# Moving the record scatters and the turning of rows by a unit in a sparse graph-attention kernel

## The chip, the cores and the metric

The kernel runs on one core of a Trainium2 chip. The metric is the device time of one execution in microseconds. The engines are TensorE (PE; its weight loads are PEld), VectorE (DVE), ScalarE (ACT), GpSimd (POOL) and SyncE (SP), which here issues transfers alone.

## The reference

A transformer convolution over a graph of 8192 nodes with a dense 0/1 adjacency matrix, and a layer norm over the sum with its input:

```python
q = (x @ Wq + bq).reshape(n, H, C)        # n = 8192, H = 4, C = 32
k, v = ...                                 # the same with Wk, bk and Wv, bv
attn = einsum('nhc,mhc->hnm', q, k) / sqrt(C)
alpha = softmax of attn over the m with adj[n, m] != 0
out = einsum('hnm,mhc->hnc', alpha, v), transposed to (n, C * H)
x_r = x @ Ws + bs
beta = sigmoid(concat([out, x_r, out - x_r]) @ Wb)
y = layernorm(x + beta * x_r + (1 - beta) * out)
```

The first rows of the matrix are full of edges, the later ones nearly empty, so the number of neighbours falls with the node number.

## The kernel before

Nodes are in 64 tiles of 128. Tile 0 is worked densely, in 40 small "pieces" strewn over the run. All others go by lists: the key and value rows of all nodes are computed first and stored in memory (`kv_rows`, 1 KB a row), and for each node only the rows of its neighbours are gathered.

**Units.** A tile's list of slots is cut into chunks of at most 24 slots; a chunk is a unit. There are 76: tile 1 has units 0 to 3 (19, 19, 18, 18 slots), tile 2 units 4 to 6, tile 3 units 7 and 8, tile 4 units 9 to 11, tile 5 units 12 and 13, tile 6 units 14 and 15 (14 and 13 slots), tile 7 unit 16 (23), tile 8 units 17 and 18, tile 9 units 19 and 20, and from there on tiles have one unit, but for tile 16. All engines run through the same list of units, each in an order written out in its own block, and meet by semaphores.

**In a unit.** POOL issues one indirect gather for each slot (L743) into a ring of 60 slots of `kv`; it waits on `summed` where a slot is still in use. DVE multiplies by the query and reduces (L1134, L1136), takes words, and after ACT's exponential (L978) weighs the values (L1156). PE sums them (L923). DVE finishes a tile in the next tile's first unit.

**Scan.** The lists come from the adjacency matrix. Along with the units, one later tile a unit is scanned: SP loads its four parts of 1 MB into a ring of five (L571, `load_adj`; each waits until ACT has masked the part five before), ACT turns them to masks (L945), PE packs them into words (L773), DVE takes the largest words out (L1167 to L1174). Unit k scans tile k + 4 on DVE, and k + 5 on ACT and PE.

**Records.** Within a window of tiles nodes are ranked by degree and change places. Windows are tiles 2 and 3 (window 0), 4 to 7 (window 1), 8 to 15 (window 2), then eight tiles each. A record holds a node's row of `x`, its list and its number. When the spots are known (`find_spots`, L1276, in unit 5 for window 1, in unit 13 for window 2), POOL scatters a window's records to memory, one indirect transfer a tile (L715), and SP loads them back by tile (L577, `load_record`) in a unit given by `load_plan`: never ahead of the scatter's unit, and not over four tiles ahead of use. A record load also waits until the store of the tile ten before has landed. POOL stores a finished tile six tiles behind (L723).

**Turning.** For the query of tile p + 1, PE transposes its rows (`turn_rows`, L795), ACT copies them (`copy_xs`, L969), PE multiplies them by the weights (`project_qr`, L800, L801), ACT copies a part (`copy_r`, L973). DVE waits for that in the first unit of tile p + 1.

**Dense pieces.** SP loads 0.5 MB of `x` columns (L581) two units ahead of a group of pieces, and one unit after its begin the values (L585) and a stretch of the adjacency matrix, `d_in` (L588), for which DVE waits in `mark_piece` (L1343). All SP loads are in one queue, in this order in a unit: `place_x` (L565, the `x` part of records, two windows ahead), records, dense loads, adjacency parts of the scan.

Of the kernel before, what the change touches and what calls it, by code (L numbers as in the profile page):

```python
# [16 lines left out]
T = N // P  # L17
# [20 lines left out]
WINDOWS = [[2, 3], [4, 5, 6, 7]] + [list(range(t, t + 8)) for t in range(8, T, 8)]  # L38
# [48 lines left out]
def chunks(p):  # L87
    n = -(-SLOTS[p] // MAX_S)
    return [SLOTS[p] // n + (c < SLOTS[p] % n) for c in range(n)]


def n_chunks(p):
    return len(chunks(p))
# [3 lines left out]
UNIT_OF = {pc: k for k, pc in enumerate(UNITS)}  # L97
# [4 lines left out]
def half(k):  # L102
    return (SIZES[k] + 1) // 2
# [68 lines left out]


def scatter_plan():
    at = {2: 0}
    for k, w in KEYS_AT.items():
        last = UNIT_OF[WINDOWS[w][0] - 1, 0] - (w > 1)
        if w + 2 < len(WINDOWS):
            last = min(last, LISTED_AT[WINDOWS[w + 2][0]] - 1)
        at[min(k + 6, last)] = w  # L180
    return at


SCATTER_AT = scatter_plan()


# [48 lines left out]
def heads_begun(k):  # L235
    return sum(h is not None for u, (c, h) in PIECE_AT.items() if u < k)
# [60 lines left out]
def sparse_tiles(nc, x, adj, Wq, bq, Wk, bk, Wv, bv, Ws, bs, Wb, kv_dram, x_cols, rec_dram, late_dram, ident, gate_w, eps_col, tile_list,  # L297
                 n_dense, n_late, w_all, b_row, bk_col, bq_col, ones, out):
    ctx = ExitStack()
    with ctx:  # L300
# [232 lines left out]
        def need(eng, sem, value):  # L533
            if value > 0:
                eng.wait_ge(sem, value)
# [217 lines left out]
        def _(pe):  # L753
# [11 lines left out]
            def pack_part(t, h):  # L765
                w, k = ps_w[t % 2], part_no(t, h)
                if h == 0:
                    need(pe, words_checked, t - 2)
                    nc.tensor.matmul(w[:], place_w[:], place[:], start=True, stop=False)
                pe.wait_ge(masked, k + 1)  # L770
                for s in range(SLABS_A_PART):
                    slab = h * SLABS_A_PART + s
                    last = nc.tensor.matmul(w[:], bit_w[:, slab], mask[:, k % 2, s * WORD:(s + 1) * WORD],  # L773
                                            start=False, stop=(slab == SLABS - 1))
                last.then_inc(part_packed, 1)
# [5 lines left out]
            def spread_keys(w):  # L781
                n = len(WINDOWS[w])
                pe.wait_ge(diag_ready, w + 1)
                pe.wait_ge(d_q_ready, 1)
                need(pe, ranked, w)
                for b in range(0, n, 4):
                    m = min(n - b, 4)
                    last = nc.tensor.matmul(ps_key[:, b * P:(b + m) * P], ones_sq[:],  # L788
                                            diag[:, b:b + m].rearrange("p a c -> p (a c)"), start=True, stop=True)
                last.then_inc(keys_spread, 1)  # L790

            def turn_rows(p):
                pe.wait_ge(rec_loaded[p % RECS], rec_loads(p))
                need(pe, xs_ready, p - 1)
                nc.tensor.transpose(ps_x[:, 0:P], rec_in[:, p % RECS, 0:D], ident[:]).then_inc(rows_turned, 1)  # L795

            def project_qr(p):
                pe.wait_ge(xs_ready, p)
                need(pe, q_used, p - 2)
                nc.tensor.matmul(ps_q[p % 2][:, 0:2 * D], ones[:], b_row[0:1, 2 * D:4 * D], start=True, stop=False)  # L800
                nc.tensor.matmul(ps_q[p % 2][:, 0:2 * D], xs[:, p % 2], w_all[:, 2 * D:4 * D], start=False,  # L801
                                 stop=True).then_inc(q_ready, 1)
# [21 lines left out]
            def turn_piece(k):  # L824
                c, h = PIECE_AT[k]
                pe.wait_ge(d_expd, head_no(c, h) + 1)
                for b in range(DKEYS // P):
                    last = nc.tensor.transpose(ps_key[:, b * P:(b + 1) * P], d_e[:, b * P:(b + 1) * P], ident[:])  # L828
                last.then_inc(d_turned, 1)

            def sum_piece(k):
                c, h = PIECE_AT[k]
                pe.wait_ge(d_wT_ready, head_no(c, h) + 1)
                pe.wait_ge(d_v_loaded, 16 * (c + 1))
                for b in range(DKEYS // P):
                    last = nc.tensor.matmul(ps_key[:, 0:C], d_wT[:, b * P:(b + 1) * P], d_v[:, b, h * C:(h + 1) * C],
                                            start=(b == 0), stop=(b == DKEYS // P - 1))
                last.then_inc(d_summed, 1)
# [60 lines left out]
            spread_keys(0)  # L899
            pack_words(4)  # L900
            for k, (p, c) in enumerate(UNITS):
                if c == 0 and p + 1 < T:
                    turn_rows(p + 1)
                scan = k in SCAN_AT and SCAN_AT[k] + 1 < T
                if scan:
                    pack_part(SCAN_AT[k] + 1, 0)
                    pack_part(SCAN_AT[k] + 1, 1)
                if c == 0 and p + 1 < T:
                    project_qr(p + 1)
                if k in RANK_AT:  # L910
                    need(pe, d_copied, heads_begun(k))
                    spread_keys(RANK_AT[k])
                if k in PIECE_AT:
                    begin_piece(k)
                if scan:
                    pack_part(SCAN_AT[k] + 1, 2)
                    pack_part(SCAN_AT[k] + 1, 3)
                piece = k in PIECE_AT and PIECE_AT[k][1] is not None
                if piece:
                    turn_piece(k)  # L920
                pe.wait_ge(weighted, k + 1)
                for s in range(SIZES[k]):
                    last = nc.tensor.matmul(acc[:, c * D:(c + 1) * D], ident[:], kv[:, START[k] + s, D:2 * D],  # L923
                                            start=(s == 0), stop=(s == SIZES[k] - 1))
                    if s in (half(k) - 1, SIZES[k] - 1):
                        last.then_inc(summed, 1)
                if piece:
                    sum_piece(k)
                if k == OVER_AT:
                    pe.wait_ge(over_ready, 1)  # L930
                    pe.wait_ge(ranked, len(WINDOWS))
                    pe.wait_ge(d_copied, H * DCHUNKS)
                    nc.tensor.matmul(ps_key[0:1, 0:T], one_col[:], over[:], start=True, stop=True).then_inc(over_summed, 1)
                if k == LOOP_AT:
                    fallback()

        @block.scalar
        def _(act):
# [117 lines left out]
            for s in range(SLABS):  # L1056
                last = nc.scalar.mul(bit_w[:, s], ident[:], float(CODE << s))
# [16 lines left out]
            for k, (p, c) in enumerate(UNITS):  # L1074
                t = SCAN_AT.get(k, T)
                scan = t + 1 < T
                if scan:
                    mask_part(t + 1, 0)
                    mask_part(t + 1, 1)
                if c == 0 and p + 1 < T:  # L1080
                    copy_xs(p + 1)
                begun, ended = PIECE_AT.get(k), PIECE_AT.get(k - 1)
                if ended and ended[1] is not None:
                    copy_sums(k - 1)
                exp_chunk(k)
                if k and UNITS[k - 1][1] == 0 and UNITS[k - 1][0] > 1:
                    normalize(UNITS[k - 1][0] - 1)
                if scan:
                    mask_part(t + 1, 2)
                    mask_part(t + 1, 3)  # L1090
                if begun and begun[1] is None:
                    copy_keys(k)
                if c == 0 and p > 1:
                    gate_exp(p - 1)
                if c == 0 and p + 1 < T:
                    copy_r(p + 1)
                if begun and begun[1] is not None:
                    exp_piece(k)
                if t < T:
                    check_words(t)  # L1100
                if begun and begun[1] is not None:
                    copy_turned(k)
                n = n_chunks(p)
                if n > 1 and c == n - 1:
                    r = p % 2
                    act.wait_ge(below_ready, multi_upto(p))
                    nc.scalar.activation(share[:, r, 0:n], below[:, r, 0:n], ACT.Exp, scale=SCALE).then_inc(share_ready, 1)
                if k in RANK_AT:
                    rank_window(RANK_AT[k])
                if k == JOIN_AT:  # L1110
                    act.wait_ge(d_low_ready, 1)
                    nc.scalar.activation(d_share[:], d_share[:], ACT.Exp).then_inc(d_share_ready, 1)
                if k == JOIN_AT + 1:
                    finish_first()
                if k == LOOP_AT:
                    fallback()
# [475 lines left out]
```

## Time and profile before

| | us |
|---|---|
| median of 3 timed runs | 1698.73 (1697.92 to 1701.44) |
| the profiled execution, own time | 1692.9 |
| its span, first to last instruction | 1691.1 |
| mean granted TensorE clock in it | 0.747 |

Rows of the timeline give start, duration, engine, line, operation, tile written and tile read, and in brackets the idle time of the engine just before and what ended it. "issue" is time in which the engine waited for nothing that the profile shows. The busy time of SP rows spans all transfers merged in a row.

### The profile page before, as it was taken

The page shows a single profiled execution, that of the slowest core. Times are in us where ns is not written, and L with a number is a line of the kernel's source. Part 1 is how long each engine was busy: PE and PEld are TensorE (multiplying, and loading weights), DVE is VectorE, ACT ScalarE, POOL GpSimd, SP SyncE. Part 2 cuts the span into 40 slices and gives each one's busy share as a digit, 9 for nine tenths or more (in the row PEclk, how much of TensorE's full clock was granted, in tenths as well). Part 3 has the DMA queues.
Part 4 walks back from the last instruction along what each step waited for, and adds up shares of the span by engine and source line. Part 5 has one row for each costly group of instructions (what it writes and reads, how often), then busy time and mean ns, then how long its engine had stood idle before and what let it go on. Part 6 is the DMA issues. An engine that isn't in the chain of part 4 may idle for free.

```text
span 1691.1 us, 19935 instructions
## 1 busy us (share of the span) xinstructions
PE 1037.8 (61%) x4648; PEld 641.3 (38%) x4708; DVE 1317.6 (78%) x3330; ACT 834.6 (49%) x1581; POOL 1203.5 (71%) x1745
## 2 busy tenths in 40 slices
PE   7405555577564365676767766776777784454564
PEld 5202323354342233343434443443454342243353
DVE  4887888889876388877867777886886888887585
ACT  2305434346645145654565657674866685331222
POOL 5265774777667776677777777777777777777774
PEclk9656767778786678777877787777787787766575
DMA  9758976769786477787699878988799798333431
GB/s 357 288 213 319 278 264 225 261 223 331 261 316 236 172 249 281 275 322 254 246 334 326 299 266 317 350 301 324 296 352 331 284 340 302 107 95 111 108 101 53
DMA packets 129220, 438.45 MB, mean 259 GB/s; under 512 B 25319, under 2 KB 60606, under 8 KB 96334
## 3 DMA queue, kind: packets, MB, share of 16 engines
q1 hardware_dynamic: 74718, 297.15, 47.4%
q0 software_dynamic: 53808, 135.83, 25.3%
q10 hardware_dynamic: 576, 4.19, 0.6%
q8 instruction: 38, 0.62, 0.1%
q14 instruction: 80, 0.66, 0.1%
HBM read 417.69 MB, written 19.44 MB: 258 GB/s over the span
## 4 chain that ended last, share of the span: by engine, by line
DVE 29%; POOL 28%; issue 16%; DVEq 9%; PE 7%; DMA 6%; ACT 3%; SPq 0%; ACTq 0%; POOLq 0%
POOL s_kv L743 24%; DVE s_raw L1136 4%; DVE s_kv L1134 4%; DVE s_wtop L1174 3%; DMA s_d_in<-in_adj 3%; DVEq L1173 3%; DVE s_kv L1156 2%; POOL node_records L715 2%; DVE s_top L1218 2%; DVEq L1323 2%; PE s_acc L923 2%; POOL out_rows L723 2%; PE s_ps_w L773 1%; DVEq L1225 1%; DVE s_d_max L1334 1%
## 5 line engine op out<-in xcount | busy, mean ns | idle before, releaser
L743 POOL DMA_INDIRECT s_kv<-kv_rows,s_rec_in x1057 | 1053.9, 997 | 396.4 <-issue 319.3
L773 PE MATMUL s_ps_w<-s_mask,s_bit_w 128*128 128x512 bf16 x1001 | 330.6, 474 | 276.6 <-ACT s_mask L945 273.7
L945 ACT ACTIVATE s_mask<-s_adj_in 128x2048 bf16<-128x2048 f32 x252 | 477.9, 1898 | 30.4 <-PE s_ps_w L773 15.8
L923 PE MATMUL s_acc<-s_kv,ident 128*128 128x128 f32 x2114 | 326.8, 326 | 122.8 <-DVE s_kv L1156 122.6
L923 PEld LDWEIGHTS s_acc<-s_kv,ident 128*128 128x128 f32 x2114 | 318.0, 241 | 147.4 <-DVE s_kv L1156 145.1
L773 PEld LDWEIGHTS s_ps_w<-s_mask,s_bit_w 128*128 128x128 bf16 x1008 | 102.6, 112 | 470.4 <-ACT s_mask L945 349.8
L1134 DVE TENSOR_TENSOR s_kv<-s_kv,s_ps_q 128x1792 f32<-128x1792 f32 (+17 forms) x76 | 152.7, 2009 | 74.9 <-DMA s_kv<-kv_rows,s_rec_in 73.1
L978 ACT ACTIVATE s_ps_q<-s_sc 128x56 f32<-128x56 f32 (+17 forms) x76 | 16.9, 222 | 347.9 <-DVE s_sc L1147 347.9
L1136 DVE TENSOR_REDUCE s_raw<-s_kv 128x56 f32<-128x1792 f32 (+17 forms) x76 | 152.6, 2007 | 5.6
L1156 DVE TENSOR_TENSOR s_kv<-s_kv,s_ps_q 128x1792 f32<-128x1792 f32 (+17 forms) x76 | 152.2, 2003 | 5.7 <-ACT s_ps_q L978 3.7
L1174 DVE MAX8 s_wtop<-s_words 128x8 f32<-128x512 f32 x171 | 118.8, 695 | 14.8 <-issue 1.3
L818 PE MATMUL s_ps_key<-s_d_kT,s_d_qT 32*128 32x512 f32 x128 | 83.6, 736 | 67.4 <-DVE s_d_pen L1343 67.4
L715 POOL DMA_INDIRECT node_records<-s_rec,s_spot x62 | 61.6, 993 | 53.0 <-DVE s_spot L1276 35.0
L969 ACT COPY s_xs<-s_ps_x 128x128 f32<-128x128 f32 x63 | 16.3, 259 | 151.4 <-PE s_ps_x L795 151.2
L723 POOL DMA_INDIRECT out_rows<-s_yout,s_rec_in x63 | 64.6, 1026 | 26.8 <-issue 17.7
L962 ACT ACTIVATE s_diag<-s_ps_key,s_neg_key 128x1024 bf16<-128x1024 f32 (+2 forms) x62 | 66.1, 1066 | 28.1 <-PE s_ps_key L788 23.8
L828 PE MATMUL s_ps_key<-ident,s_d_e 128*128 128x128 f32 x256 | 49.0, 354 | 46.8 <-ACT s_d_e L1009 46.8
L1218 DVE MAX8 s_top<-s_cand 128x8 f32<-128x72 f32 (+6 forms) x234 | 62.4, 267 | 17.5 <-issue 1.5
L1170 DVE MATCH_REPLACE8 s_words<-s_wtop,s_words 128x512 f32<-128x512 f32 x108 | 73.0, 676 | 0.0
L1009 ACT ACTIVATE s_d_e<-s_ps_key,s_d_shift 128x1024 f32<-128x1024 f32 x32 | 35.6, 1114 | 74.1 <-DVE s_d_shift L1336 74.1
L828 PEld LDWEIGHTS s_ps_key<-ident,s_d_e 128*128 128x128 f32 x256 | 39.1, 183 | 69.0 <-ACT s_d_e L1009 68.9
L800 PE MATMUL s_ps_q<-b_row,ones 1*128 1x256 f32 x126 | 49.3, 473 | 18.1 <-ACT s_xs L969 18.1
(258 smaller groups left out, 1469.1 us busy)
## 6 DMA issues: line engine op xcount, KB each, us to landing
s_adj_in<-in_adj SPq DMA_DIRECT2D x248, 1024.0 KB, 8.1
s_kv<-kv_rows,s_rec_in POOLq DMA_INDIRECT x1057, 5.6
kv_rows<-s_kv SPq DMA_DIRECT2D x16, 512.0 KB, 7.6
s_rec_in<-node_records SPq DMA_DIRECT2D x62, 106.0 KB, 6.7
s_kv<-in_x_cols SPq DMA_DIRECT2D x4, 1024.0 KB, 8.5
s_adj_in<-in_adj ACTq DMA_DIRECT2D x4, 1024.0 KB, 15.8
s_d_in<-in_x_cols SPq DMA_DIRECT2D x8, 512.0 KB, 8.9
s_d_v<-kv_rows SPq DMA_DIRECT2D x8, 512.0 KB, 10.2
```

Source lines behind the costliest of these rows:

```text
L715: nc.gpsimd.indirect_dma_start(out=rec_dram[:, :], out_offset=bass.IndirectOffsetOnAxis(ap=spot[:, t:t + 1], axis=0), in_=rec[:, w % 2, j] ...
L723: nc.gpsimd.indirect_dma_start(out=out[:, :], out_offset=bass.IndirectOffsetOnAxis(ap=rec_in_u[:, r, NODE_AT:NODE_AT + 1], axis=0), in_=y_ ...
L743: nc.gpsimd.indirect_dma_start(out=kv[0:n, START[k] + s], out_offset=None, in_=kv_dram[:, :], in_offset=bass.IndirectOffsetOnAxis(ap=rec_i ...
L773: last = nc.tensor.matmul(w[:], bit_w[:, slab], mask[:, k % 2, s * WORD:(s + 1) * WORD], start=False, stop=(slab == SLABS - 1))
L828: last = nc.tensor.transpose(ps_key[:, b * P:(b + 1) * P], d_e[:, b * P:(b + 1) * P], ident[:])
L923: last = nc.tensor.matmul(acc[:, c * D:(c + 1) * D], ident[:], kv[:, START[k] + s, D:2 * D], start=(s == 0), stop=(s == SIZES[k] - 1))
L945: nc.scalar.activation(mask[:, q % 2], adj_in[:, q % ADJ_RING], ACT.Sign, accum_out=edges[:, t, h:h + 1]).then_inc(masked, 1)
L1134: nc.vector.tensor_tensor(part, part, ps_q[r][:, 0:D].unsqueeze(1).to_broadcast([P, s, D]), ALU.mult)
L1136: nc.vector.tensor_reduce(raw[:, 0:s * H].rearrange("p (s h) -> p s h", h=H), part.rearrange("p s (h c) -> p s h c", h=H), AX, ALU.add)
L1156: nc.vector.tensor_tensor(v, v, e_sh.unsqueeze(3).to_broadcast([P, s, H, C]), ALU.mult).then_inc(weighted, 1)
L1174: nc.vector.max(got[:, 8 * k:8 * k + 8], words[:])
L1218: nc.vector.max(got[:, 8 * k:8 * k + 8], all_cand)
```

## The change

Three windows are scattered one unit later, in the unit just ahead of the window's own first unit: window 0 in unit 3 (was 2), window 1 in unit 8 (was 7), window 2 in unit 16 (was 15). The record loads of `load_plan` follow: tiles 4 to 7 in SP's unit 8 (was 7), tiles 8 to 10 in unit 16 (was 15). The places of all later windows stay. The turning of the next tile's rows with its copies goes from a tile's first unit to its last; where a tile has one unit nothing moves.

```diff
 def scatter_plan():
-    at = {2: 0}
+    at = {UNIT_OF[2, 0] - 1: 0}
     for k, w in KEYS_AT.items():
-        last = UNIT_OF[WINDOWS[w][0] - 1, 0] - (w > 1)
+        last = UNIT_OF[WINDOWS[w][0], 0] - 1
         if w + 2 < len(WINDOWS):
             last = min(last, LISTED_AT[WINDOWS[w + 2][0]] - 1)
         at[min(k + 6, last)] = w
...
             for k, (p, c) in enumerate(UNITS):
-                if c == 0 and p + 1 < T:
+                ends = c == n_chunks(p) - 1 and p + 1 < T
+                if ends:
                     turn_rows(p + 1)
...
-                if c == 0 and p + 1 < T:
+                if ends:
                     project_qr(p + 1)
...
-                if c == 0 and p + 1 < T:
+                ends = c == n_chunks(p) - 1 and p + 1 < T
+                if ends:
                     copy_xs(p + 1)
...
-                if c == 0 and p + 1 < T:
+                if ends:
                     copy_r(p + 1)
```

## Rows read from the trace of the kernel before

**Rows 1.** The page, part 1: busy time, share and instructions of each engine.

```profile
PE 1037.8 (61%) x4648; PEld 641.3 (38%) x4708; DVE 1317.6 (78%) x3330; ACT 834.6 (49%) x1581; POOL 1203.5 (71%) x1745
```

**Rows 2.** The page, part 5: groups; busy, mean ns, idle before and releaser.

```profile
L743 POOL DMA_INDIRECT s_kv<-kv_rows,s_rec_in x1057 | 1053.9, 997 | 396.4 <-issue 319.3
...
L800 PE MATMUL s_ps_q<-b_row,ones 1*128 1x256 f32 x126 | 49.3, 473 | 18.1 <-ACT s_xs L969 18.1
```

**Rows 3.** Timeline of POOL, 60 to 600 us.

```profile
131.40 1.02 POOL L715 DMA_INDIRECT node_records<-s_rec,s_spot  x1 [10.71 <-DVE s_spot L1276]
...
163.12 0.99 POOL L743 DMA_INDIRECT s_kv<-kv_rows,s_rec_in  x1 [5.88 <-PE s_acc L923]
...
269.22 0.88 POOL L743 DMA_INDIRECT s_kv<-kv_rows,s_rec_in  x1 [7.50 <-PE s_acc L923]
...
283.42 1.04 POOL L715 DMA_INDIRECT node_records<-s_rec,s_spot  x1 [12.12 <-DVE s_spot L1276]
...
338.93 1.03 POOL L743 DMA_INDIRECT s_kv<-kv_rows,s_rec_in  x1 [0.30 <-issue]
...
472.11 1.03 POOL L715 DMA_INDIRECT node_records<-s_rec,s_spot  x1 [12.15 <-DVE s_spot L1276]
...
575.22 1.03 POOL L723 DMA_INDIRECT out_rows<-s_yout,s_rec_in  x1 [0.30 <-issue]
```

**Rows 4.** Waits of POOL, whole run: total us, times, longest.

```profile
POOL s_kv L743 <- PE s_acc L923: 31.8, 9, 9.2
```

**Rows 5.** Timeline of POOL, 680 to 700 us.

```profile
692.30 1.00 POOL L743 DMA_INDIRECT s_kv<-kv_rows,s_rec_in  x1 [9.23 <-PE s_acc L923]
```

**Rows 6.** Timeline of DVE, 60 to 600 us.

```profile
151.65 2.69 DVE L1156 TENSOR_TENSOR s_kv<-s_kv,s_ps_q 128x2432 f32<-128x2432 f32 x1 [2.16 <-ACT s_ps_q L978]
...
221.15 0.75 DVE L1343 TENSOR_SCALAR s_d_pen<-s_d_in 128x1024 bf16<-128x1024 f32 x1 [0.19 <-DMA s_d_in<-in_adj]
...
375.00 2.42 DVE L1134 TENSOR_TENSOR s_kv<-s_kv,s_ps_q 128x2176 f32<-128x2176 f32 x1
...
420.53 1.23 DVE L1334 TENSOR_REDUCE s_d_max<-s_ps_key 128x1 f32<-128x1024 f32 x1 [0.34 <-PE s_ps_key L820]
...
503.86 1.89 DVE L1134 TENSOR_TENSOR s_kv<-s_kv,s_ps_q 128x1664 f32<-128x1664 f32 x1 [4.08 <-DMA s_kv<-kv_rows,s_rec_in]
...
584.19 0.69 DVE L1343 TENSOR_SCALAR s_d_pen<-s_d_in 128x1024 bf16<-128x1024 f32 x1 [22.56 <-DMA s_d_in<-in_adj]
```

**Rows 7.** Timeline of SP, 60 to 600 us.

```profile
138.46 0.97 SPq L577 DMA_DIRECT2D s_rec_in<-node_records  x2
...
195.84 5.05 SPq L588 DMA_DIRECT2D s_d_in<-in_adj  x1
...
305.90 5.18 SPq L577 DMA_DIRECT2D s_rec_in<-node_records  x4
...
577.59 0.33 SPq L577 DMA_DIRECT2D s_rec_in<-node_records  x1
```

**Rows 8.** Timeline of PE, 140 to 160 us.

```profile
150.70 0.47 PE L795 MATMUL s_ps_x<-ident,s_rec_in 128*128 128x128 f32 x1 [11.54 <-DMA s_rec_in<-node_records]
```

**Rows 9.** Windows: length, busy by engine (instructions), PEclk, DMA share, GB/s.

```profile
120.00:132.00 12.00, 1.62 (x3) 0.66 (x3) 8.00 (x33) 2.89 (x6) 1.29 (x2) 0.50 0.07 22
...
138.00:144.00 6.00, 0.98 (x3) 0.31 (x4) 4.36 (x9) 3.85 (x5) 4.77 (x5) 0.86 1.00 365
```

**Rows 10.** The page, part 6: issues, KB each, us to landing.

```profile
s_adj_in<-in_adj SPq DMA_DIRECT2D x248, 1024.0 KB, 8.1
```

**Rows 11.** The page, part 3: packets, MB, share of 16 engines' span.

```profile
q0 software_dynamic: 53808, 135.83, 25.3%
```

**Rows 12.** Timeline of SP, 312 to 340 us.

```profile
322.83 9.30 SPq L571 DMA_DIRECT2D s_adj_in<-in_adj  x4
```

**Rows 13.** All record loads of L577, whole run.

```profile
DMA to landing us min/median/max: 2.1/6.7/17.7
```

**Rows 14.** Timeline of SP, 500 to 532 us.

```profile
512.28 2.22 SPq L571 DMA_DIRECT2D s_adj_in<-in_adj  x2
```

## The prediction

> **What bounds the kernel now.** I read the page first. Its busy shares [rows 1] name DVE (1317.6 us) ahead of POOL (1203.5 us), so they would send the reader to DVE. The timeline of POOL corrects this. POOL works off one list: 1057 gathers, 62 scatters, 63 stores, each about 1.0 us busy with 0.3 us of issue behind it [rows 2]; that is 1182 x 1.3 = 1537 us, and the list starts at 71 us. So POOL is occupied almost without a hole, and its holes are worth listing. Three of them stand before the first scatter of a window, which waits for the spots that DVE computes: 10.71, 12.12 and 12.15 us [rows 3]. The waits for buffers (PE's sums) make 31.8 us in nine pieces [rows 4]; the last is the one of 9.23 us that ends at 692.30 [rows 5], and from there the list runs to the end. What moves that gather moves the end, one for one.
>
> Next I asked what sets 692.30. From 131 us on DVE waits for no gather until unit 15, where it waits 4.08 us (503.86) [rows 6], so from 472.11 on POOL sets the pace. At 575.22 POOL issues the store of tile 2 [rows 3]; SP stands before the record load of tile 12 until that store has landed (577.59) [rows 7], behind it is the adjacency piece `d_in`, and DVE waits 22.56 us for it, to 584.19 [rows 6]. From there DVE is busy up to the wait at 692.30. So the chain is: POOL's list at 472.11, store, SP, `d_in`, DVE, POOL again. Between 131 and 472 us the reverse holds: DVE is nearly without a hole, and POOL is the one that waits.
>
> **The change, part by part: the scatters.** Nothing is removed; the places are, by unit: window 0 from 2 to 3, window 1 from 7 to 8, window 2 from 15 to 16. Later windows keep theirs (k + 6 is the smaller number there).
>
> *Window 2.* POOL now issues the 13 gathers of unit 15 where it waited 12.15 us. They take 13 x 1.3 = 16.9 us and their buffers have been free since unit 11. The wait goes whole: -12.15 us, and unit 16 starts that much sooner. For every us by which POOL reaches unit 15 later than now, one us of it is lost.
>
> *Window 1.* The 12.12 us go too (19 of unit 7's 20 gathers need only unit 4). From the last wait of unit 6 (269.22) it would work through units 6 to 8 and reach unit 9, tile 4, at about 327 instead of 338.93 [rows 3]. This gains nothing by itself: unit 15 is after the records of tile 4, and they are what is late next, below.
>
> *Window 0.* POOL gathers unit 2 at 121 to 144.4 (18 x 1.3), and scatters at 144.4 instead of 131.4. Unit 3 then needs the first sums of unit 0.
>
> **The turning of rows.** `turn_rows(2)` stands today ahead of all of unit 0 on PE, and waits 11.5 us for records to 150.70 [rows 8]; ACT's `copy_xs(2)` and its exponential stand behind it, and DVE waits 2.16 us for that [rows 6]. With the turning in unit 3 DVE is 2.15 us earlier. Nine turnings move (tiles 2 to 7, 9, 10 and 17, each behind a tile of several units). Each is a transpose, two products (the first takes 49.3 us for 63 tiles, so 0.8 us each [rows 2]) and two ACT copies: under 2 us of PE, covered by DVE's long units. The one place without cover is unit 11, where DVE already waits 0.34 us for PE's scores [rows 6]: +1.7 us there, on DVE only.
>
> **What SP does meanwhile.** Behind the record loads of tiles 2 and 3 SP has `place_x(2)`, the dense columns, and all adjacency loads from number 21 on. They get through at 138.46 now, 5.7 us after the second scatter starts at 132.7 [rows 7]; they will at 145.8 + 5.7 = 151.5, 13 us later. ACT and PE have loaded parts for that time, but the DMA engines don't: their share is 1.00 at 138 to 144 [rows 9], and the half megabyte issued at 195.84 is still 25.3 us on its way [rows 6, 7]. The last loads issued before SP stops should be in by about 148 (one takes 8.1 us [rows 10], and they queue); the next bytes come at about 153. About 5 us of DMA time are lost. Given back are the gathers of unit 2, of which 10 now run at 121 to 132, where the engines are 0.07 busy [rows 9]; less what POOL gains later about 5 gathers fewer lie before the critical load, at 0.253 x 1691 / 1182 = 0.36 us each [rows 11] that is 1.9 us. The critical load is the first `d_in` of adjacency: issued 195.84, used 221.15, with 0.19 us to spare [rows 6, 7]. I put its landing 5.0 - 1.9 = 3.1 us later, and DVE's and SP's clock from there on at +3.1 us instead of -2.15. Bounds: -2.15 (the load is in time) and +8 (no relief, the 5 us lost, and 3 us more because what moves behind gathers then moves slowly, as that load's 25.3 us show).
>
> **Records of tile 4.** Their loads move from SP's place for unit 7 to that for unit 8, that is past four adjacency loads that wait for ACT. Today they are issued at 305.90 [rows 7]; the four loads they move behind are at 322.83 to 332.1 [rows 12], so with `place_x(3)` they start at 332.6. The line's landing times are 2.1, 6.7 and 17.7 us (least, median, most) [rows 13]; with two whole adjacency parts just ahead I take 9.0. That is 341.6, against 338.93 for POOL's unit 9 today: POOL is 2.7 us late there, plus the 3.1. The bounds: +0.4 at the median, +11.4 at the most. POOL's gain of 12 us from window 1 is spent entirely in this wait. DVE is not touched by this: it comes to unit 9 at 375.00 [rows 6], when its 17 gathers (22 us) are long in.
>
> [...]
>
> **Records of tile 8.** They too move past four adjacency loads, whose last goes out at 514.2 [rows 14]. It waits for ACT, ACT for DVE's unit 15, and that loses its wait of 4.1 us for gathers: the record load goes at 514.2 + 0.4 - 4.1 + 3.1 + 1.7 = 515.3 and lands at 524.3. POOL comes to unit 17 today at 472.11 + 45 x 1.3 = 530.6 (8 scatters, 36 gathers, a store), so at 530.6 - 12.15 + 5.8 = 524.2. 0.1 us.
>
> **Sum.** -12.15 + 3.1 + 2.7 + 0.1 = -6.2 us, at unit 17. After this the order of work is that of today, the store of tile 2 and all behind it come 6.2 us earlier, and so does the end. The profiled execution took 1692.9 us with a span of 1691.1; it would take 1686.7. The runs timed have a median of 1698.73, 5.8 us above it; the same step from there gives 1692.5 us.
>
> **Rivals.** (a) The dense load is in time after all, and the records land at the median: -12.15 - 2.15 + 0.4 + 0.3 = -13.6 us, 1685.1. For it: the engines idle before 132, and the transfer has slack that the trace can't show. Against: 0.19 us of slack on DVE. (b) The move is a wash: SP's 13 us of silence cost 8 us at the dense load, and tile 4's records take 11 us: -12.15 + 8 + 4.7 = +0.5, 1699.3. The busy shares speak for such a result too, read simply: DVE is the fullest engine, so waits of POOL cost nothing. The Trainium skill (Perfetto Trace Analysis, Identifying Performance Opportunities) says to take the engine of highest occupancy first; by that rule the change leaves the time at 1698.7. The issue gaps, which busy time leaves out, speak against it. (c) Slower: SP's ring is so full at unit 9 that the records take the 17.7 us that this line has shown once, on top of the late dense load: -12.15 + 8 + 11.4 + 0.4 = +7.7 us, 1706.4. It decides from the point where the two delays exceed 12.15 us together. Against it: at 305 to 340 the adjacency loads are paced by ACT, not by the ring.
>
> **How the numbers follow.** Forecast 0.42, (a) 0.22, (b) 0.20, (c) 0.16. The measurement tells 0.2%, 3.4 us, from nothing. Faster by more: all of (a), nine tenths of the forecast, a little of (b): 0.61. Slower by more: (c) and a little of (b): 0.18. Within: 0.21. The range runs from (a) with its record loads a little quicker, 1684, over the forecast's 1692.5, to the upper side of (b), 1701; what is left out is (c) and the edges. The forecast's own range is 1688 to 1697.
>
> **What the changed profile would show.** No wait of POOL on `s_spot` above 1 us; a wait of some 14 us of POOL at unit 9 for tile 4's records, its first gather at 342 to 347; SP's record loads at about 151, 335 and 513; the first `s_d_pen` after a wait of 3 to 6 us, instead of 0.19; scatter of window 2 starting at 480 to 484; unit 16 done 5 to 9 us earlier, and so the gather now at 692.30; POOL without a hole from there. I am wrong if `s_d_pen` shows no wait (then (a)), if POOL waits more than 20 us at unit 9, if PE's `turn_rows` blocks unit 16, or if DVE's long stretch before 692 doesn't move with the store of tile 2.

## The result, and the profile after

The changed kernel takes 1692.94 us (median of 12 runs, 1692.02 to 1695.27) against 1699.74 us for the kernel before (12 runs, 1695.23 to 1703.59) on the same chip: a ratio of 0.9957, 95% interval 0.9947 to 0.9968, or 7.3 us less (5.4 to 9.0). A second measurement of both kernels gave 0.995 (0.9937 to 0.9963). The forecast was 1692.5 us. Ratios and spreads leave out runs over 1.5% above a kernel's fastest (one of 1770.21 us in experiment 2, two of the kernel before in experiment 7).

The profiled execution of the changed kernel took 1695.27 us with a span of 1693.4, so beside the profile of before (1692.9, span 1691.1) it looks 2.3 us slower. That contradiction is the first thing to clear up, and a second profile of the unchanged kernel does it (first experiment). Here are the rows that answer to those of before (the edit makes the file longer, so L924, L1136, L1278, L1336 and L1345 are L923, L1134, L1276, L1334 and L1343 of the kernel before). First the timeline of GpSimd (POOL) in the changed kernel:

```profile
144.55 1.02 POOL L715 DMA_INDIRECT node_records<-s_rec,s_spot  x1 [0.30 <-issue]
...
156.61 1.04 POOL L743 DMA_INDIRECT s_kv<-kv_rows,s_rec_in  x1 [9.72 <-PE s_acc L924]
...
304.66 1.02 POOL L715 DMA_INDIRECT node_records<-s_rec,s_spot  x1 [0.31 <-issue]
...
347.31 1.03 POOL L743 DMA_INDIRECT s_kv<-kv_rows,s_rec_in  x1 [13.54 <-DMA s_rec_in<-node_records]
...
485.54 1.02 POOL L715 DMA_INDIRECT node_records<-s_rec,s_spot  x1 [0.30 <-issue]
...
530.73 1.03 POOL L743 DMA_INDIRECT s_kv<-kv_rows,s_rec_in  x1 [4.04 <-DMA s_rec_in<-node_records]
...
575.65 1.04 POOL L723 DMA_INDIRECT out_rows<-s_yout,s_rec_in  x1 [0.30 <-issue]
...
693.65 1.00 POOL L743 DMA_INDIRECT s_kv<-kv_rows,s_rec_in  x1 [9.60 <-PE s_acc L924]
```

The three waits for spots ahead of the scatters (10.71, 12.12 and 12.15 us in [rows 3]) are gone. Three longer waits stand in their place: GpSimd waits for TensorE's sums at 156.61 (9.72 us, where window 0's wait was), for the records of tile 4 at 347.31 (13.54 us, where window 1's was) and for those of tile 8 at 530.73 (4.04 us). For window 2's 12.15 us only this last one stands, and it is smaller. All waits for sums together grow from 31.8 us [rows 4] to 52.0.

The timeline of VectorE (DVE), the same run, at the rows of [rows 6]. The `s_d_pen` rows are `mark_piece`, which waits for the dense adjacency load `d_in`:

```profile
228.15 0.74 DVE L1345 TENSOR_SCALAR s_d_pen<-s_d_in 128x1024 bf16<-128x1024 f32 x1 [9.27 <-DMA s_d_in<-in_adj]
...
429.54 1.22 DVE L1336 TENSOR_REDUCE s_d_max<-s_ps_key 128x1 f32<-128x1024 f32 x1 [2.94 <-PE s_ps_key L820]
...
585.00 0.69 DVE L1345 TENSOR_SCALAR s_d_pen<-s_d_in 128x1024 bf16<-128x1024 f32 x1 [22.93 <-DMA s_d_in<-in_adj]
```

And that of SyncE (SP), at the rows of [rows 7]:

```profile
153.27 1.04 SPq L577 DMA_DIRECT2D s_rec_in<-node_records  x2
...
204.77 1.60 SPq L588 DMA_DIRECT2D s_d_in<-in_adj  x1
...
339.51 2.89 SPq L577 DMA_DIRECT2D s_rec_in<-node_records  x4
...
520.19 11.52 SPq L577 DMA_DIRECT2D s_rec_in<-node_records  x4
```

The record loads sit where the forecast put them (about 151, 335 and 513 us), 2 to 7 us later. The first `s_d_pen` now has 9.27 us of wait where [rows 6] show 0.19, and starts 7.0 us later. Read against that one profile this says that the late dense load cost 7 us. A second profile of the kernel before puts the same row at 226.94 us, later than in one of the two profiles of the changed kernel, so that reading doesn't stand; what the load's place did cost is taken up in experiment 2.

### The profile page after: what moved, and what is told of

The parts are those of the page before. It is cut to its first block, busy times and chain, and to the rows that moved or that the text cites. A ratio compares the mean times of both kernels' runs of the same rounds, so it can differ in the third digit from the quotient of the medians.

```text
span 1693.4 us, 19995 instructions
## 1 busy us (share of the span) xinstructions
PE 1065.1 (63%) x4708; PEld 646.7 (38%) x4708; DVE 1315.9 (78%) x3330; ACT 834.4 (49%) x1581; POOL 1205.2 (71%) x1745
## 4 chain that ended last, share of the span: by engine, by line
POOL 34%; DVE 24%; issue 17%; DVEq 8%; DMA 7%; PE 7%; ACT 3%; SPq 0%; POOLq 0%; ACTq 0%
POOL s_kv L743 29%; DVE s_raw L1138 3%; DVE s_kv L1136 3%; DVE s_wtop L1176 3%; DVEq L1175 3%; DMA s_d_in<-in_adj 3%; POOL node_records L715 2%; DMA s_adj_in<-in_adj 2%; POOL out_rows L723 2%; DVE s_kv L1158 2%; PE s_acc L924 2%; DVE s_top L1220 1%; PE s_ps_w L773 1%; DVEq L1325 1%; DVE s_d_max L1336 1%
## 5 line engine op out<-in xcount | busy, mean ns | idle before, releaser
L773 PE MATMUL s_ps_w<-s_mask,s_bit_w 128*128 128x512 bf16 x1008 | 341.5, 484 | 271.7 <-ACT s_mask L946 271.4
L946 ACT ACTIVATE s_mask<-s_adj_in 128x2048 bf16<-128x2048 f32 x252 | 478.0, 1899 | 62.2 <-DMA s_adj_in<-in_adj 48.2
L924 PE MATMUL s_acc<-s_kv,ident 128*128 128x128 f32 x2114 | 327.1, 326 | 112.5 <-DVE s_kv L1158 112.2
L924 PEld LDWEIGHTS s_acc<-s_kv,ident 128*128 128x128 f32 x2114 | 318.2, 241 | 138.9 <-DVE s_kv L1158 136.5
L773 PEld LDWEIGHTS s_ps_w<-s_mask,s_bit_w 128*128 128x128 bf16 x1008 | 102.8, 113 | 479.3 <-ACT s_mask L946 358.9
L1136 DVE TENSOR_TENSOR s_kv<-s_kv,s_ps_q 128x1792 f32<-128x1792 f32 (+17 forms) x76 | 152.7, 2009 | 73.2 <-DMA s_kv<-kv_rows,s_rec_in 71.2
L1220 DVE MAX8 s_top<-s_cand 128x8 f32<-128x72 f32 (+6 forms) x234 | 62.3, 266 | 17.5 <-issue 1.5
```

The costliest lines, as they stand in the source:

```text
L946: nc.scalar.activation(mask[:, q % 2], adj_in[:, q % ADJ_RING], ACT.Sign, accum_out=edges[:, t, h:h + 1]).then_inc(masked, 1)
L1136: nc.vector.tensor_tensor(part, part, ps_q[r][:, 0:D].unsqueeze(1).to_broadcast([P, s, D]), ALU.mult)
```

## The experiments

All ratios are to the kernel before, run in turn with it on the same chip. Where times of the changed kernel's trace are compared, they are those of its second profile (experiment 1), unless said otherwise. The changed kernel was not timed beside experiments 3 to 6, which ran on another chip than 1 and 2, so a difference of theirs to the changed kernel is one of two ratios, each with its own interval.

**1. Both kernels once more.** No edit; the control.

> The kernel before, unchanged, for a second profiled execution. Theory A (the first profiled execution, 1692.9 us, was a quick one by chance, and its chain is otherwise typical): timed ratio 1.000, profiled execution at 1697 to 1701; the 5 to 8 us are then found at one or two transfers. Rival B (the profiler shortens this kernel): profiled execution again near 1693, and the chain the same to a microsecond.

> The changed kernel, unchanged, for a second profiled execution. In the first one POOL's unit 17 began at 530.73, against 530.37 in the kernel before, though the timed runs are 7 us quicker. Theory A: timed ratio 0.996, the wait of DVE for the first adjacency piece (9.27 us) and the waits for records (13.54 and 4.04 us) come back within 3 us each. Rival B: these waits differ widely from execution to execution (by more than 5 us), and the timed gain is where they are short.

Measured: the kernel before against itself 1.0007 (0.9991 to 1.0024); the changed kernel 0.995 (0.9937 to 0.9963), 1690.45 us to 1697.48. The two new profiles have spans of 1701.1 and 1689.2 us. This is the pair to compare; the timelines of the kernel before, second profile, VectorE and then SyncE:

```profile
226.94 0.69 DVE L1343 TENSOR_SCALAR s_d_pen<-s_d_in 128x1024 bf16<-128x1024 f32 x1 [5.87 <-DMA s_d_in<-in_adj]
...
509.66 1.89 DVE L1134 TENSOR_TENSOR s_kv<-s_kv,s_ps_q 128x1664 f32<-128x1664 f32 x1 [4.06 <-DMA s_kv<-kv_rows,s_rec_in]
```

```profile
201.76 0.79 SPq L588 DMA_DIRECT2D s_d_in<-in_adj  x1
```

The same program, unchanged, has 5.87 us of wait at the first `s_d_pen` in one execution and 0.19 in the other. Why, its ScalarE (ACT) timeline shows, here the second profile of the kernel before:

```profile
178.99 1.91 ACT L945 ACTIVATE s_mask<-s_adj_in 128x2048 bf16<-128x2048 f32 x1 [2.64 <-DMA s_adj_in<-in_adj]
...
185.67 1.91 ACT L945 ACTIVATE s_mask<-s_adj_in 128x2048 bf16<-128x2048 f32 x1 [4.68 <-DMA s_adj_in<-in_adj]
...
192.69 1.91 ACT L945 ACTIVATE s_mask<-s_adj_in 128x2048 bf16<-128x2048 f32 x1 [3.03 <-DMA s_adj_in<-in_adj]
...
198.82 1.91 ACT L945 ACTIVATE s_mask<-s_adj_in 128x2048 bf16<-128x2048 f32 x1 [4.12 <-DMA s_adj_in<-in_adj]
```

Between 150 and 205 us the adjacency parts arrive later than ScalarE wants them (six waits, 18.0 us in sum; the first profile has one, of 3.60 us, at 201.32). SyncE gets to the dense load at 201.76 instead of 195.84 [rows 7], and the 6 us stay: tile 4's first gather starts at 344.7 (338.93 in [rows 3]) and the last wait for sums ends at 700.97 (692.30 in [rows 5]). The profile on which the forecast was built was of an execution in which that stream of loads ran ahead. Neither profile of the kernel before is a typical one: its timed runs have medians of 1695.91 to 1699.74, the first profiled execution (1692.9) is quicker than every timed run of the result above, and the second (1702.89) is the slowest of its ten.

The rows of the changed kernel's second profile, GpSimd, at tile 8's first gather and at the last wait for sums:

```profile
527.19 1.03 POOL L743 DMA_INDIRECT s_kv<-kv_rows,s_rec_in  x1 [1.90 <-DMA s_rec_in<-node_records]
...
690.38 1.00 POOL L743 DMA_INDIRECT s_kv<-kv_rows,s_rec_in  x1 [9.79 <-PE s_acc L924]
```

With the second pair, milestone by milestone (us, from the timelines; the last row is the execution's span):

| | before | changed | difference |
|---|---|---|---|
| first `s_d_pen` | 226.94 | 226.13 | -0.8 |
| spots of window 1 | 288.20 | 287.29 | -0.9 |
| first gather of unit 9 (tile 4) | 344.7 | 345.66 | +1.0 |
| spots of window 2 | 476.94 | 476.90 | 0.0 |
| first gather of unit 17 (tile 8) | 536.2 | 527.19 | -9.0 |
| store of tile 2 | 581.04 | 572.02 | -9.0 |
| third dense chunk, `s_d_pen` | 590.79 | 581.20 | -9.6 |
| last wait for sums ends | 700.97 | 690.38 | -10.6 |
| span | 1701.1 | 1689.2 | -11.9 |

In this pair nothing is gained or lost up to 477 us, 9.0 us are gained between 477 and 527, and they are carried to the end through the chain that the forecast named. The pair overstates the gain, since its execution of the kernel before took longer than the median one: the spans differ by 11.9 us, against the first profile of the kernel before by only 1.9 (1691.1 to 1689.2), and the timed runs (7.3 and 8.5 us) lie between. So the pair shows where the gain is made, and the timed runs how large it is.

**2. The windows apart.** Windows 1 and 2 later, window 0 back in unit 2:

```
-    at = {UNIT_OF[2, 0] - 1: 0}
+    at = {2: 0}
```

> The changed kernel with window 0 scattered in unit 2 as before. Theory A (SP's silence of 13 us costs DVE 9.27 us at the first adjacency piece, and all of it reaches the end by way of tile 4's records): that wait falls below 2 us, unit 9 starts at about 339 instead of 347, and the time is 10 us below the kernel before, ratio 0.994. Rival B (the delay is made good before unit 15): as the changed kernel, 0.996.

Window 0 alone later, windows 1 and 2 back:

```
-        last = UNIT_OF[WINDOWS[w][0], 0] - 1
+        last = UNIT_OF[WINDOWS[w][0], 0] - 1 - (w in (1, 2))
```

> Windows 1 and 2 scattered as before, window 0 in unit 3, the turnings moved. Theory A: DVE waits about 9 us at the first adjacency piece and is 7 us late from there, so the spots of window 2 come at 478 instead of 471, and the time is 7 us above the kernel before, ratio 1.004. Rival B (POOL is 8 us ahead after unit 2, and DVE makes the wait good): ratio 0.998 to 1.000.

Measured: 0.9962 (0.9947 to 0.9977) and 1.0016 (1.0003 to 1.0029). Without window 0's move the gain is the same as with it, within the intervals. Window 0 and the turning alone make the kernel slower, by 2.6 us (1700.04 to 1697.48), between the two numbers expected and just clear of noise. The first `s_d_pen`, on the timelines of VectorE of the one and of the other:

```profile
227.20 0.88 DVE L1345 TENSOR_SCALAR s_d_pen<-s_d_in 128x1024 bf16<-128x1024 f32 x1 [8.49 <-DMA s_d_in<-in_adj]
```

```profile
226.72 0.74 DVE L1345 TENSOR_SCALAR s_d_pen<-s_d_in 128x1024 bf16<-128x1024 f32 x1 [7.86 <-DMA s_d_in<-in_adj]
```

SyncE issues the first record loads at 138.74 us in the first and at 153.64 in the second; the dense load lands at the same time, to 0.5 us. So in these executions SyncE's silence of 15 us costs the dense load nothing. VectorE waits 2 to 2.6 us longer there than in the kernel before (5.87 us), about the 2.15 us that the moved turning gives it.

Where the 2.6 us of the second kernel come from its profile doesn't show: the last wait for sums ends at 699.40, against 700.97 and 692.30 in the two profiles of the kernel before. The spread of the timed runs gives a hint. With window 0 in unit 2 they lie 7.0 to 10.3 us apart (the kernel before, the first kernel here, the one of experiment 3; 9 to 31 runs each). With window 0 in unit 3 they lie 3.3 to 4.9 us apart (the changed kernel twice, the second kernel here, experiments 5 and 6; 6 to 12 runs each), and 7.7 us in experiment 4, where the load itself is moved. That would fit a dense load that is in time in some executions of the kernel before, as in its first profile, and always late in the other; window 0's move would then take the quick executions away. It is not shown, and it is not all, for beside the moves of windows 1 and 2 window 0's costs nothing (1690.45 to 1691.33 us).

**3. Window 2 alone later**, windows 0 and 1 back, the turning as changed.

```
-    at = {UNIT_OF[2, 0] - 1: 0}
+    at = {2: 0}
-        last = UNIT_OF[WINDOWS[w][0], 0] - 1
+        last = UNIT_OF[WINDOWS[w][0], 0] - 1 - (w == 1)
```

> The changed kernel with windows 0 and 1 scattered where the kernel before has them (units 2 and 7); window 2 in unit 16 and the turning of rows stay changed. Theory (the whole gain is the 12 us wait of GpSimd at window 2, now filled with unit 15's gathers): GpSimd still waits 10.7 and 12.2 us at windows 0 and 1, not at window 2; the records of tile 4 are loaded by 312 us, and the time is 0.9950 to 0.9960 of the kernel before, as for the whole change, or about 1 us less than that. Rival (windows 0 and 1, or the turning of rows, carry part of the gain): 0.998 or more.

Measured: 1691.53 us to 1695.91, ratio 0.9971 (0.9958 to 0.9984). The waits of GpSimd (reason, total us, times, longest):

```profile
POOL s_kv L743 <- PE s_acc L924: 39.8, 17, 10.7
POOL node_records L715 <- DVE s_spot L1278: 22.6, 2, 11.9
```

Two waits for spots are left, the window 2 one is gone, and about two thirds of the gain are there (-4.9 us, interval -2.7 to -7.1, against -7.3). It is less than the 0.9950 to 0.9960 expected, and the intervals overlap, so whether the moves of windows 0 and 1 add 1 or 2 us to it, or nothing, is not settled by this run.

**4. The disputed term alone: the first dense load earlier.** The changed kernel, with SyncE's order in unit 2 changed:

```
-                if k - 1 in PIECE_AT and PIECE_AT[k - 1][1] is None:
+                if k - 1 in PIECE_AT and PIECE_AT[k - 1][1] is None and k - 1 > FIRST_PIECE:
                     load_dense_rows(PIECE_AT[k - 1][0])
+                if k == FIRST_PIECE:
+                    load_dense_rows(0)
```

> The changed kernel with the first dense adjacency load (L588, tile s_d_in) issued by SyncE before unit 2's adjacency loads, not behind them. This is the disputed term of the prediction (+3.1 us for a late first dense load) measured by itself. Theory A (a late load there moves all that follows on VectorE, as the 6 us between two executions of the kernel before seemed to do): VectorE's wait of 7.6 to 9.3 us at the first s_d_pen falls below 3 us, window 2's spots come 5 to 8 us earlier, and the time falls by 4 to 7 us against the changed kernel, a ratio of 0.991 to 0.993 to the kernel before. Theory B (what VectorE gains there it loses at the 22.9 us wait for the third dense load, which hangs on tile 2's store and so on GpSimd): the wait goes, and the ratio stays at 0.995 to 0.996. Rival C (the adjacency loads of unit 2 come late instead): no gain in the wait's end, 0.996 to 0.999.

Measured: 1684.26 us, ratio 0.9919 (0.9897 to 0.9941). On VectorE's timeline:

```profile
218.71 0.69 DVE L1347 TENSOR_SCALAR s_d_pen<-s_d_in 128x1024 bf16<-128x1024 f32 x1
```

The wait is gone, the row starts 7.4 us earlier than in the changed kernel's second profile (226.13), and theory A holds: the store of tile 2 comes 5.3 us earlier (566.74 to 572.02), the last wait for sums 5.0 us (685.38 to 690.38), and the time falls by about 5 us (0.995 to 0.9919 of 1696; the two intervals overlap slightly, 0.9937 and 0.9941). The way goes by VectorE's spots of window 2 (470.78 to 476.90) and by tile 4's first gather (337.50 to 345.66), and not by the third dense chunk, whose wait stays at 22.89 us and comes earlier with the store. So the forecast was right that this load sets VectorE's clock; that window 0's move delays it shows only against the quick first profile, and the timed runs of experiment 2 leave it open.

**5. The records one unit earlier in SyncE's order**, where the kernel before has them:

```
-        k = max(scattered[WINDOW_OF[p]], UNIT_OF[max(p - LEAD, 1), 0])
+        k = max(scattered[WINDOW_OF[p]] - (WINDOW_OF[p] in (1, 2)), UNIT_OF[max(p - LEAD, 1), 0])
```

> The changed kernel with SyncE's first record loads of windows 1 and 2 taken one unit earlier in its own order (units 7 and 15, where the kernel before has them), still behind the scatters' landing by their semaphore; this undoes only the term that the prediction put at +2.7 us. Theory: the records of tile 4 are loaded by 320 us, not 338; GpSimd's wait of 13.8 us at unit 9 falls to 1 to 8 us and that of 1.9 us at unit 17 goes. What is then late next is window 2's spots on VectorE at 477 us, so of the 13.8 us some 6 to 8 are kept: the time falls by 3 to 8 us against the changed kernel, a ratio of 0.991 to 0.993. Rival (the adjacency loads that now stand behind the record loads feed the marking late, and VectorE loses what GpSimd gains): 0.995 or more.

Measured: 1684.07 us, ratio 0.9922 (0.99 to 0.9944). SyncE's loads go out at 310.29 (337.60 in the changed kernel's second profile), and of GpSimd's waits for records none is left (one of 8.18 us for TensorE's sums at 401.73 is new); what is left at window 2 is, on GpSimd's timeline:

```profile
479.05 1.02 POOL L715 DMA_INDIRECT node_records<-s_rec,s_spot  x1 [1.79 <-DVE s_spot L1278]
...
681.86 1.00 POOL L743 DMA_INDIRECT s_kv<-kv_rows,s_rec_in  x1 [9.22 <-PE s_acc L924]
```

The scatter of window 2 starts 5.0 us earlier (484.02 to 479.05) and is again bound by the spots; the last wait for sums ends 8.5 us earlier (690.38 to 681.86). This is the price of the late records: about 5 us of time (0.995 to 0.9922 of 1696, with intervals that overlap slightly), of the 12 that window 1's move had won.

**6. The dense loads ahead of the record loads of the same unit.** In unit 17 this takes the third dense adjacency out from behind tile 12's record load, which waits for the store of tile 2:

```
-                for p in LOAD_AT.get(k, []):
-                    load_record(p)
                 if k + 2 in PIECE_AT and PIECE_AT[k + 2][1] is None:
                     load_dense_x(PIECE_AT[k + 2][0])
                 if k - 1 in PIECE_AT and PIECE_AT[k - 1][1] is None:
                     load_dense_rows(PIECE_AT[k - 1][0])
+                for p in LOAD_AT.get(k, []):
+                    load_record(p)
```

> The changed kernel with SyncE's dense loads (L581, L585, L588) issued ahead of the record loads of the same unit, so that in unit 17 the third dense adjacency does not stand behind tile 12's record load, which waits for the store of tile 2. Theory: VectorE's wait of 22.9 us at the second s_d_pen behind that store (584 us) falls below 10 us, and with it GpSimd's waits of 7.9 and 9.8 us for TensorE near 650 and 690 us; the time falls by 5 to 15 us against the changed kernel, a ratio of 0.986 to 0.993. Rival (VectorE is only as far as GpSimd's gathers let it be; its waits for the gathers' landing, 71.8 us in total, grow by what the wait gave back): the wait goes and the ratio stays at 0.995 to 0.996.

Measured: 1673.89 us, ratio 0.9867 (0.9845 to 0.9889), the fastest kernel of the study: 22 us below the kernel before and about 14 below the changed one. The timelines of SyncE and of VectorE:

```profile
542.10 0.62 SPq L588 DMA_DIRECT2D s_d_in<-in_adj  x1
```

```profile
561.09 0.69 DVE L1345 TENSOR_SCALAR s_d_pen<-s_d_in 128x1024 bf16<-128x1024 f32 x1
```

The load goes out at 542.10 instead of 575.25, and the wait of 22.86 us is gone. GpSimd's waits near 644, 664 and 690 us (5.6, 3.3 and 9.8 us in the changed kernel's second profile) are gone too (none above 0.4 us there), and VectorE's for gathers grow by only 3 us (71.8 to 74.9 in sum). The gather that started at 690.38 starts at 674.31, so nearly all of the 17.5 us between the two spans is made here, though the edit reorders later units as well. The largest wait on the chain was one that the change did not touch.

**7. Four kernels on a slower chip.** The edits of 4, 5 and 6 together; the kernel before with those of 4 and 6; the turning of rows moved alone (`at = {2: 0}` and `- (w in (1, 2))` in the changed kernel); window 1 alone later (`at = {2: 0}` and `- (w == 2)`).

> The changed kernel with the three edits of SyncE's order together: the first dense adjacency ahead of unit 2's adjacency loads, the record loads of windows 1 and 2 one unit earlier, and the dense loads ahead of the record loads of their unit. Alone they gave ratios of 0.9919, 0.9922 and 0.9867 where the change itself gives 0.995 to 0.9957. Theory (three separate waits of three stretches, so the gains add: 0.0034 + 0.0031 + 0.0086 beside the change's own 0.9953): 0.979 to 0.982. Rival (the dense load of unit 17 and the records of window 2 release the same stretch, and one gain swallows the other): 0.983 to 0.987. In the trace VectorE has no wait above 3 us at the first and at the third s_d_pen and GpSimd none above 3 us for records.

> The kernel before with the same two edits of SyncE's order of dense loads (its record loads of windows 1 and 2 stand in units 7 and 15 already); beside the run above this gives what the change is worth once the other waits are out of its way. Theory (the change is worth the whole of window 2's 12 us and of window 1's, where GpSimd sets the pace): 0.986 to 0.989, so that the change is worth 0.006 to 0.009 on top, more than the 0.0045 that it is worth in the kernel as it stands. Rival (what the change gives was hidden in VectorE's waits that the edits take away): within 0.003 of the run above.

> Only the second part of the change: the next tile's rows turned in a tile's last unit; all windows scattered as in the kernel before. Theory (a step of TensorE and ScalarE that GpSimd and VectorE don't wait for in either place, but for some 2 us before the keys' maximum in unit 11): 0.999 to 1.001, with that wait of 1.8 to 3 us there. Rival (the part carries some of the gain): 0.998 or less. Second rival (the 2 us in unit 11 reach the end): 1.0012 to 1.002.

> Window 1 alone scattered later (unit 8), windows 0 and 2 as in the kernel before, turning changed. This is the term of +2.7 us by itself (records of tile 4 wanted after a wait of 14 us where there were 12 at the scatter). Theory: GpSimd's wait of 12 us at window 1 goes, one of 13 to 14.5 us for the records of tile 4 stands in its place, tile 4's first gather starts 0.5 to 3 us later than in the kernel before, and the ratio is 1.000 to 1.002. Rival (the gathers brought ahead free VectorE earlier and win back what the records lose): below 0.999.

These four ran on another chip than the rest, and there the kernel before itself took 2154.27 us, 27% more than on the others. The ratios are 0.996 (0.9932 to 0.9988), 0.9983 (0.995 to 1.0017), 1.004 (1.0012 to 1.0068) and 1.0093 (1.0062 to 1.0124). None of the four is in the range that its theory gave. The expected numbers were worked out from the faster chips' profiles, so the misses say little about those chips. Why, the waits of VectorE in the kernel with the turning alone show (reason, total us, times, longest):

```profile
DVE s_divisor L1307 <- remote: 145.2, 12, 31.8
DVE s_d_max L1336 <- remote: 106.8, 9, 32.4
DVE s_top L1220 <- issue: 68.7, 47, 3.2
```

None of these is there on the other chips (1.5 us at L1220; no "remote" at all). The single instructions of GpSimd and VectorE take what they took: 997 ns for a gather, 2009 for the product at L1136; TensorE's at L773 take 500 ns, where the changed kernel's second profile has 489. Between them GpSimd, VectorE, ScalarE and TensorE stand idle with "issue" or "remote" as the reason, for which the profile names no instruction or transfer of this core, and GpSimd is no longer full: it waits 160.2 us in sum for TensorE's sums, where the changed kernel's second profile has 50.3. With the bound elsewhere, a wait removed from GpSimd should be worth less, and the kernel with all edits gains 0.4% where the change with one of them gained 1.3%; that the one is the cause of the other is not shown. What holds the instructions the profile doesn't name; it stays open. So does whether the gains of experiments 4 to 6 add up on a chip like the others, what the change is worth beside them, and what the turning of rows costs by itself there: the runs that were to tell did not. On this chip the turning alone costs 0.4%, clear of noise. On the others no run separates it from window 0's move, and the two together cost 0.16% (experiment 2), so a cost of the turning is not ruled out.

One reading can be made within this chip. Window 1 alone later is 0.7% slower than the turning alone by the medians (2177.86 to 2163.61 us), 0.5% by the ratios, whose intervals just overlap. The timelines of GpSimd at tile 4's first gather, first with window 1 later, then with the turning alone:

```profile
390.25 1.03 POOL L743 DMA_INDIRECT s_kv<-kv_rows,s_rec_in  x1 [26.25 <-DMA s_rec_in<-node_records]
```

```profile
383.90 1.02 POOL L743 DMA_INDIRECT s_kv<-kv_rows,s_rec_in  x1 [11.54 <-PE s_acc L924]
```

Two waits, of 12.91 us for spots (at 317.16) and of 11.54 for sums, are exchanged for one of 26.25 for records, and the gather starts 6.4 us later. Here the exchange loses; on the faster chips it was nearly even (12.23 for 13.79).

## Why the prediction was right, point by point

**The gain is window 2's wait: right.** Experiment 3 keeps two thirds of the gain with that window alone (with the turning moved); the milestones of experiment 1 show it between the spots of window 2 and unit 17. GpSimd did follow its list from there without a hole until the wait for sums.

**The chain to the end: right.** The 9.0 us at unit 17 are 9.0 at the store of tile 2, 9.6 at the dense chunk that waits for it, 10.6 at the last wait for sums. Experiment 6 cuts this chain at the load and wins 14 us more, which shows it the other way round. VectorE was the fullest engine by busy time, the change took waits from GpSimd, and the time fell by 0.4%. The Trainium skill (Perfetto Trace Analysis, Identifying Performance Opportunities) says to optimize the engine of highest occupancy first, which is VectorE here, with 78% to GpSimd's 71%. The measured gain of 7.3 us from GpSimd's waits doesn't agree with a plain reading of it, though experiment 6 won more at a wait of VectorE.

**+3.1 us for window 0's silence on SyncE: the term whose size the runs don't bear out.** In the second pair it measured 0 within 1 us: the first `s_d_pen` is at 226.94 in the kernel before and at 226.13, 226.72 and 227.20 in three kernels with window 0 in unit 3, in unit 3 and in unit 2. Against the first profile of the kernel before it would be 5.0 to 7.0 us (221.15 to 226.13 and 228.15). By timed runs it is nothing beside the other two moves, and with the turning alone beside it the kernel is 2.6 us slower (experiment 2). So the size is not settled. The step behind it was "with 0.19 us to spare": the load was taken as just in time, from a profile in which it was. In three of the four profiles on these chips with window 0 in unit 2 it is 6 us late (226.94, 227.20, 227.24), behind adjacency loads that are short of supply themselves, and against these the lost DMA time changes nothing. The lower bound of this term, -2.15 us, shows in none of them: VectorE's 2 us from the moved turning end up in the wait. The wait itself was 7.64 and 9.27 us, where the forecast had 3 to 6.

**+2.7 us for tile 4's records: mechanism right, size near.** The wait came (13.54 and 13.79 us; forecast some 14) and swallowed window 1's 12 us. Net, unit 9 starts 1.0 us later, not 2.7. The whole cost of their late place is larger than the term, since without it part of window 1's gain is kept: 5 us, by experiment 5. The landing time that was taken, 9.0 us, was about right: 345.66 less 337.60 is 8.1 us for the first of the four.

**+0.1 us for tile 8's records: 1.9 us** (4.04 in the first profile), because the loads went out at 516.60 and not at 515.3 and the first landed 10.6 us after that, not 9.0. GpSimd came to them at 525.3, 1.1 us later than reckoned.

**+1.7 us at unit 11: right in place and about right in size** (waits of 1.85 and 2.94 us for a forecast of some 2), and without effect on window 2's spots in the second pair (476.90 to 476.94). It isn't there in every kernel with the turning moved: the first kernel of experiment 2 and those of experiments 3 and 6 wait 0.36 to 0.45 us at that place, as the kernel before does.

**The sum** was -12.15 + 3.1 + 2.7 + 0.1 = -6.2; the second pair gives -12.0 + 0 + 1.0 + 1.9 = -9.1 at unit 17, and the timed runs -7.3 and -8.5. Window 2's scatter started at 485.54 and 484.02, where the forecast had 480 to 484. The forecast time, 1692.5, was nearer than its terms were, and in that there is luck: a base of 1698.73 that was 1 us low made up for a gain that was about 1 us small. By size the case lies between the forecast and rival (a), but none of (a)'s three parts (dense load in time, -2.15 from the turning, records at the median) came out as written: the load was waited for 7.64 us, the 2.15 us ended in that wait, and the records took 8.1 us.

## What to carry to other kernels

Before a term is built on a slack of tenths of a microsecond, look whether what feeds it has slack, and take a second profile: here a load that was just in time behind a stream of loads was 6 us late in the next execution of the same kernel, and against that execution a delay put on it cost nothing. When a wait is filled with other work, look in the same place for the next thing that the engine needs, and move its load too; here the records' loads, moved back one unit, gave about 5 us beside the change's 7. And the largest wait on the chain (22.9 us at a load queued behind another load's wait) was a matter of the order of a few lines on SyncE's queue, worth 14 us; follow the chain for such a place first.

## What the runs showed of the hardware

The same program, with the same instructions, differs by 6 us at 227 us into the run from how fast 1 MB loads arrive (ScalarE waited 3.6 us for them in one profile and 18.0 in the other between 150 and 205 us). The difference doesn't go away: it is 8.7 us at the last wait for sums, and the two profiled executions took 1692.9 and 1702.89 us. A single pair of profiles showed the sign of this change wrong (+2.3 us), while 12 timed runs of each told it within 0.1%.

On one chip all of the kernels took some 27% longer, with unchanged durations of the single instructions of GpSimd, VectorE and ScalarE (997 ns a gather, 2009 the product at L1136, 1900 the mask at L946) and a granted TensorE clock of 0.67 to 0.69 in place of 0.73 to 0.75; waits of up to 32 us on VectorE that the profile puts down to "remote" and to nothing of this core stood between them. The cause was not found.
